# Source tiles of two message-passing layers cut at span bounds instead of group bounds, in a four-layer graph network on Trainium2

## What is computed

```python
# layer 0: per source node, mean of the attributes of its edges, then three dense layers with batch norm
v_e = segment_sum(edge_attr, src) / max(count(src), 1)
# layer 1
agg = segment_sum(x[src], dst) / max(count(dst), 1);  relu((agg + x) @ W.T + b)
# layer 2: messages by edge type
agg = segment_sum(([x[src], x[dst]] @ Wmsg[type] + bmsg[type]), dst) / max(count(dst), 1)
h = [x, agg] @ Wupd + bupd;  x + gelu(norm(h) * gamma + beta)
# layer 3
out = segment_sum((x @ W)[row] * dinv[row] * w * dinv[col], col) + b;  batch_norm(relu(out))
```

## Time and profile before

| | |
|---|---|
| median of 3 runs | 3748.39 us (3743.72 to 3750.21) |
| the profiled execution | 3743.15 us, its span 3741.4 us |
| PE, DVE, ACT, POOL busy | 75%, 67%, 41%, 49% of the span |
| scatter of the edges (POOL, L750) | up to about 1108 us |
| reduce(0) | about 1108 to 1363 us |
| gather(1) with its scatters | about 1468 to 1807 us |
| gather(2), reduce(2) | about 2176 to 2984 us |
| gather(3) with its scatters | about 3078 to 3424 us |

### The profile page before, as it was taken

How to read it: one execution, slowest core, us unless ns; L and a number is a source line. 1 busy time by engine, 2 the same in 40 slices (tenths; PEclk the granted TensorE clock), 3 DMA queues, 4 the chain that set the end, 5 groups by cost and what they waited for, 6 DMA issues and landing times.

```text
span 3741.4 us, 94994 instructions
## 1 busy us (share of the span) xinstructions
PE 2820.6 (75%) x23282; PEld 2453.3 (66%) x23283; DVE 2495.4 (67%) x7099; ACT 1517.8 (41%) x4312; POOL 1847.8 (49%) x2243
## 2 busy tenths in 40 slices
PE   8555544444439986887799689999999958887996
PEld 6232322222229975777799479999899957776995
DVE  7666666666647778555577777777666777554667
ACT  0111100000004445555577543222365348886765
POOL 4777777777763341777433354444521007774000
PEclk9999999999999997999899899999999989998998
DMA  6444444444448943778698035555378807885883
GB/s 216 150 150 141 149 143 146 147 143 149 141 131 285 292 144 104 279 274 280 216 293 274 9 115 175 177 179 183 126 241 248 263 30 273 272 283 194 289 286 123
DMA packets 419041, 721.75 MB, mean 193 GB/s; under 512 B 68624, under 2 KB 198169, under 8 KB 417932
## 3 DMA queue, kind: packets, MB, share of 16 engines
q1 hardware_dynamic: 330492, 494.35, 42.7%
q0 software_dynamic: 88464, 226.43, 16.1%
HBM read 481.26 MB, written 285.09 MB: 205 GB/s over the span
## 4 chain that ended last, share of the span: by engine, by line
PE 42%; POOL 23%; issue 13%; DMA 11%; DVE 5%; ACT 3%; SPq 2%; DVEq 2%; POOLq 1%; ACTq 0%
PE ps L1375 20%; POOL slots L750 19%; PE ps L1408 9%; DMA gbuf<-ring_raw,to_blk 8%; PE ps L1410 5%; POOL gbuf L804 3%; DMA ring_raw<-gbuf 2%; PE ps L1420 2%; PE ps L1250 2%; PE ps L1461 1%; DVEq L501 1%; PE ps L1452 1%; DVE stats L1935 1%; SPq L501 1%; ACT ring_raw L976 1%
## 5 line engine op out<-in xcount | busy, mean ns | idle before, releaser
L804 POOL DMA_INDIRECT gbuf<-ring_raw,to_blk x774 | 754.4, 975 | 727.4 <-DVE ring_raw L1868 257.9
L750 POOL DMA_INDIRECT slots<-ring_raw,idx_edges x782 | 751.4, 961 | 242.2 <-issue 242.2
L1375 PE MATMUL ps<-ring_raw,memory 128*128 128x128 f32 (+2 forms) x6576 | 784.6, 279 | 82.6 <-DVE memory L1836 49.2
L1375 PEld LDWEIGHTS ps<-ring_raw,memory 128*128 128x128 f32 x6576 | 764.5, 193 | 104.9 <-issue 56.3
L1836 DVE TENSOR_TENSOR memory<-dst_lane,lane_ids 128x512 f32<-128x512 f32 x774 | 535.1, 692 | 74.8 <-POOL dst_lane L768 51.7
L1286 PE MATMUL ps<-memory 128*49 128x343 bf16 (+6 forms) x784 | 263.5, 489 | 387.9 <-DVE memory L1732 386.6
L1408 PE MATMUL ps<-memory 128*128 x2752 | 497.8, 273 | 9.9 <-DVE memory L1877 7.5
L1846 DVE TENSOR_TENSOR memory<-memory,ps 128x128 f32 (+2 forms) x1032 | 294.6, 285 | 308.3 <-PE ps L1375 294.8
L935 ACT ACTIVATE memory<-lane_ids,dst_lane 128x128 f32<-128x128 f32 x1032 | 330.3, 392 | 403.2 <-PE ps L1375 246.1
L1410 PE MATMUL ps<-memory 128*128 x2752 | 477.4, 220 | 0.0
L1286 PEld LDWEIGHTS ps<-memory 128*49 128x49 bf16 x784 | 113.9, 159 | 530.4 <-DVE memory L1732 301.6
(11 more groups left out here) (283 smaller groups left out, 4781.6 us busy)
## 6 DMA issues: line engine op xcount, KB each, us to landing
ring_raw<-gbuf SPq DMA_DIRECT2D x669, 268.0 KB, 3.6
ring_raw<-in_edge_attr SPq DMA_DIRECT2D x111, 448.0 KB, 3.8
ring_raw<-slots SPq DMA_DIRECT2D x153, 272.0 KB, 4.1
zr<-lane_rows SPq DMA_DIRECT2D x87, 384.0 KB
zt<-lane_rows SPq DMA_DIRECT2D x87, 384.0 KB
memory<-lane_rows SPq DMA_DIRECT2D x84, 384.0 KB, 4.8
memory<-slots SPq DMA_DIRECT2D x105, 272.0 KB, 4.1
memory<-gbuf SPq DMA_DIRECT2D x105, 268.0 KB, 3.8
```

The source lines that it names most:

```text
L750: pool.indirect_dma_start(edges, bass.IndirectOffsetOnAxis(idx_edges[0:n, u, j:j + 1], 0), edge_rows[0:n, u, j, :], None).then_inc(scatter ...
L804: pool.indirect_dma_start(gbuf, bass.IndirectOffsetOnAxis(to_blk[:, t:t + 1], 0), node_rows[:, r, :], None, bounds_check=NBLK - 1, oob_is_ ...
L1375: ins = pe.matmul(bank(r % 3, width), hots[:, r, j * P:(j + 1) * P], rows[:, j, 0:width], start=j == 0, stop=j == BLK - 1)
```

## The change

In layers 1 and 3 the gather keeps its 258 products of a tile with a group, now called **steps**, but a PSUM bank, an SBUF row and a scatter belong to a **span**: 128 consecutive blocks, whatever groups they are of. There are `SPANS` = 210 of them, in 35 rounds of six. Steps of different groups that meet in one span add up in its bank; the one-hots of blocks of other groups are zero. Because the bank of a step is now data, PE gets for each step a 16-bit word that holds the group's address, the bank, and the number of the next bank, and for each two steps a count of sends to wait for; 27 such values (three rounds) come in one register load. Before the four products of a step, PE does a one-column matmul with `start=True` on the next bank (`new_bank`), so that the products can all be `start=False`. ACT's payload copy in reduce(0) goes to a place by span (its address from a register, twelve loaded for two rounds), and one more copy keeps the target block of each tile; ACT in gather reads the count to wait for from a table, 30 to a load. The payload gets a ninth number, `P_TYPED` (source plus 128 times type less 1), which makes rows of `slots` 137 numbers wide for 136, and POOL keeps both lane tables at once; the four long POOL instructions L792 and L793 after reduce(0) go, three short ones for `to_span` come, and the whole chain waits for the last product of reduce(0). DVE makes the new tables (`span_tables`) behind `at_ready`. Layer 2 keeps its tiles.

```diff
+SPANS = -(-MAXB // P)
+SR = SPANS // RING
+SROUNDS = 3
+SWORDS = RING + RING // 2
+SENDS = 5
...
+STAGED = {1: 0, 2: SPANS, 3: SPANS + TILES}
+
+
 def sends_before(layer):
-    return RR * (layer - 1)
+    return (0, SR, SR + RR, SR + RR + SR)[layer - 1]
...
-PAY = 8
-P_ONE, P_TYPE, P_W, P_DST, P_SRC, P_TO = 0, 1, 4, 5, 6, 7
+PAY = 9
+LIST = PAY - 1
+P_ONE, P_TYPE, P_W, P_DST, P_SRC, P_TYPED, P_TO = 0, 1, 4, 5, 6, 7, 8
...
+            steps.link(pool.tensor_scalar(pay8[:, :, P_TYPED], type_i, float(P), -float(P), ALU.mult, ALU.add))
+            pool.wait_ge(pays_ready, 7)
+            pool.tensor_tensor(pay8[:, :, P_TYPED], pay8[:, :, P_TYPED], pay8[:, :, P_SRC], ALU.add).then_inc(pays_ready, 1)
...
+                        if q == 0:
+                            pool.tensor_tensor(lane_pair[:, :, t * BLK:(t + 1) * BLK],
+                                               rows[:, :, D + P_SRC:D + P_TYPED + 1].rearrange("p k w -> p w k"),
+                                               back[:, q, t:t + 1][:, :, None].broadcast_to([P, 2, BLK]), ALU.add).then_inc(kept, 1)
...
+            pool.wait_ge(products, RING + TILES)
...
-            for t, by in ((0, -P), (2, P)):
-                part = B[:, 0:TILES * BLK].rearrange("p (t k) -> p t k", k=BLK)
-                steps.link(pool.tensor_scalar(part, key_s[:, :, :, P_TYPE + t], float(by), None, ALU.mult))
-                steps.link(pool.tensor_tensor(lane_f, lane_f, part, ALU.add))
...
+            pool.tensor_copy(lanes_t[:, :], edge_w).then_inc(lanes_ready, 1)
+            unused = away[:, 1, 0:SPANS]
+            steps.link(pool.tensor_scalar(unused, key_s[:, :, 0, P_ONE], -NOWHERE, NOWHERE, ALU.mult, ALU.add))
+            steps.link(pool.tensor_tensor(unused, unused, key_s[:, :, 0, P_TO], ALU.add))
+            steps.link(pool.tensor_copy(to_span, unused))
...
+                to = to_blk if layer == 2 else to_span
...
-                for i in range(RR):
+                for i in range(RR if layer == 2 else SR):
...
+            def pay_places(h, n=2 * RING):
+                return nc.values_load_multi_w_load_instructions(
+                    at_pay[:, bass.ds(h * 2 * RING, n)], engines=[ACT_E], min_val=0, max_val=(SPANS - 1) * BLK * PAY,
+                    skip_runtime_bounds_check_because="the tables hold addresses within their tensors")[1]
...
+                    act.copy(to_of[:, bass.ds(i * RING + r, 1)], rows[:, 0, D + P_TO:D + P_TO + 1])
+                    act.wait_ge(pays_kept, i * RING + (RING + r))
+                    act.copy(pays_raw[:, bass.ds(at[r], BLK * PAY)].rearrange("p (k w) -> p k w", k=BLK),
                              rows[:, :, D:ROW_A]).then_inc(pays_kept, 1)
...
+                def counts_of(h):
+                    return nc.values_load_multi_w_load_instructions(
+                        span_steps[layer][:, bass.ds(h * SENDS * RING, SENDS * RING)], engines=[ACT_E], min_val=0,
+                        max_val=RING + GATHERED[3] + TILES,
+                        skip_runtime_bounds_check_because="the tables hold counts of a semaphore")[1]
+
+                def send_round(i, counts):
                     for r in range(RING):
                         at = i * RING + r
-                        act.wait_ge(gathered, i * RING + (RING + base + r + 1))
+                        act.wait_ge(gathered, counts[r])
...
+                counts = counts_of(0)
+                for q in range(SENDS):
+                    send_round(q, counts[q * RING:(q + 1) * RING])
+                with act.Fori(1, SR // SENDS) as h:
+                    counts = counts_of(h)
+                    for q in range(SENDS):
+                        send_round(h * SENDS + q, counts[q * RING:(q + 1) * RING])
...
+                def new_bank(to):
+                    pe.matmul(ps_flat[:, to], ident_h[:, :], none_h, start=True, stop=True, skip_group_check=True)
+
+                def step_words(h, rounds=SROUNDS):
+                    v = nc.values_load_multi_w_load_instructions(
+                        step_lists[layer][:, bass.ds(h * SROUNDS * SWORDS, rounds * SWORDS)], engines=[PE], min_val=0,
+                        max_val=65535, skip_runtime_bounds_check_because="words of 16 bits")[1]
+                    return [v[q * SWORDS:(q + 1) * SWORDS] for q in range(rounds)]
+
+                def in_bounds(v, top):
+                    return nc.s_assert_within(v, 0, top, skip_runtime_bounds_check_because="the words are built so")
+
+                def gather_steps(i, words):
                     for r in range(RING):
+                        at = in_bounds((words[r] & 0x1F8) * 16, (GROUPS - 1) * D)
+                        to = in_bounds(words[r] & 0xE00, (RING - 1) * 512)
+                        upon = in_bounds((words[r] & 7) * 512, (RING - 1) * 512)
+                        if r % 2 == 0:
+                            pe.wait_ge(staged, words[RING + r // 2])
+                        new_bank(bass.ds(upon, 1))
                         pe.wait_ge(src_hots, i * RING + (base + r + 1))
-                        pe.wait_ge(staged, i * RING + (base + r + 1))
                         for j in range(BLK):
-                            ins = pe.matmul(bank(r)[:, j * P:(j + 1) * P], hots[:, r, j * P:(j + 1) * P],
-                                            nodes[:, bass.ds(at[r], D)], start=True, stop=True)
+                            ins = pe.matmul(ps_flat[:, bass.ds(to + j * D, D)], hots[:, r, j * P:(j + 1) * P],
+                                            nodes[:, bass.ds(at, D)], start=False, stop=j == BLK - 1,
+                                            skip_group_check=True)
                         ins.then_inc(gathered, 1)
...
+                    new_bank(slice(0, 1))
+                    with pe.Fori(0, RR // SROUNDS) as h:
+                        for q, words in enumerate(step_words(h)):
+                            gather_steps(h * SROUNDS + q, words)
+                    rest = RR // SROUNDS
+                    for q, words in enumerate(step_words(rest, RR % SROUNDS)):
+                        gather_steps(rest * SROUNDS + q, words)
...
+            groups_on = bank(5, TILES)
+            mark(dve.tensor_scalar(back[:, 0, :], groups_on, -float(P), float(P), ALU.mult, ALU.add))
+            mark(dve.tensor_scalar(at_sum[:, 0, :], groups_on[0:1], float(AW), -float(AW), ALU.mult, ALU.add))
+            mark(dve.tensor_scalar(word_f, groups_on, 8.0, -8.0, ALU.mult, ALU.add))
...
+            def span_tables():
+                link(dve.tensor_scalar(turn_i, span_f, 171.0, None, ALU.mult))
+                link(dve.tensor_scalar(turn_i, turn_i, 10, None, ALU.arith_shift_right))
+                link(dve.tensor_copy(turn_f[:, 1, :], turn_i))
+                link(dve.scalar_tensor_tensor(out=turn_f[:, 0, :], in0=turn_f[:, 1, :], scalar=-float(RING), in1=span_f,
+                                              op0=ALU.mult, op1=ALU.add))
+                link(dve.scalar_tensor_tensor(out=word_f, in0=turn_f[:, 0, :], scalar=512.0, in1=word_f,
+                                              op0=ALU.mult, op1=ALU.add))
+                link(dve.tensor_scalar(turn_f[:, 1, :], turn_f[:, 0, :], RING - 1.5, -float(RING), ALU.is_gt, ALU.mult))
...
+                for layer in (1, 3):
+                    mark(dve.tensor_copy(step_parts[layer][:, :, 0:RING], word_f[32:33].rearrange("p (i r) -> p i r", r=RING)))
+                    mark(dve.tensor_scalar(step_parts[layer][:, :, RING:SWORDS],
+                                           span_f[32:33].rearrange("p (i q two) -> p i q two", q=RING // 2, two=2)[:, :, :, 1],
+                                           float(STAGED[layer] + 2), None, ALU.add))
+                link(dve.tensor_tensor(need_f, tile_ids[:, :], bank(6, TILES), ALU.add))
+                for layer in (1, 3):
+                    mark(dve.tensor_scalar(span_steps[layer], need_f[64:65], float(RING + GATHERED[layer]), None, ALU.add))
+                wait(chain.last())
```

More of the change, by code:

```diff
@@ L58 @@
 HALVES = 2 * RR
+SPANS = -(-MAXB // P)
[3 more added lines that the diff above has]
+SENDS = 5
+assert SR * RING == SPANS and SR % SENDS == 0 and RR % SROUNDS and SPANS + GROUPS - 1 == TILES and SPANS * P <= NBLK
+assert all((t * 171) >> 10 == t // RING for t in range(SPANS))
 SCALAR_HOTS = ((5,), (2, 5), (5,), (2, 5))
@@ L497, in tile_cols @@
         def tile_cols(table, k, i, n=RING, span=RING):
-            return table[0:1, k, bass.ds(i * span, n)] if k is not None else table[0:1, bass.ds(i * span, n)]
+            return table[:, k, bass.ds(i * span, n)] if k is not None else table[:, bass.ds(i * span, n)]
         def loaded(table, k, i, engine, top, span=RING):
@@ L989, in send, with send_typed, send_tiles @@
                     act.wait_ge(lane_rows_out, 32)
[L990 to L995 removed]
+                counts = counts_of(0)
[5 more added lines that the diff above has]
+                        send_round(h * SENDS + q, counts[q * RING:(q + 1) * RING])
+            def send_typed():
```

(14 more changed lines are left out.)

189 lines of the change are left out of this document (102 added, 87 removed).

## The result

The changed kernel takes 4010.26 us (median of 4 runs, 4008.34 to 4013.30) against 3746.32 us before: a ratio of 1.0704, 95% interval 1.0686 to 1.0723. Forecast were 3645 us and a gain. Where the 264 us are is seen in the profiled execution (span 4006.9 us) by stages.

The account below looks back on a forecast made before the run. PE was taken to bound reduce(0), POOL the two gathers at 1.27 us a scatter. Terms -51.5 - 51.5 - 5 + 5 = -103 us took the profiled 3743.15 to 3640, so a median of 3645; range 3605 to 3710.

Parts of the forecast that it names:

- Scatters: Gathers: POOL sends 210 for 258 a layer; as the bound it would need 278 us.
- Rival A: Gathers: new_bank and loads hide better, PE needs 259 us, POOL's 278 decide; median 3619, chance 14%.
- PE's step: Gathers: four products 0.89 us plus new_bank 0.11 make 1.00 us a step, 258 us a layer.
- Register loads: Gathers, PE: 15 loads of 27 values a layer, 1.2 us of pause each, 18 us, bounds 11 and 45.
- seven a layer, each at most 3 us, and the six banks cover that: Gathers: ACT's loads of 30 counts for five rounds would be covered by the six banks.
- PE's registers: Gathers, PE's queue: register work and issue take about 0.85 us a step, hidden behind the step's 1.00.
- the half-way case to rival B: Gathers: PE's queue slightly longer than the products, a step of 1.08 to 1.20 us; median 3670 to 3715, 15%.
- rival B: Gathers: PE's queue becomes the bound, 1.4 us a step, 385 us a layer; median 3833, chance 6%.
- reduce(0), +5: reduce(0): ACT's extra copies and loads +4 us (0 to 25), wider rows of slots +1; together +5.
- Rival C: reduce(0): ACT's register loads hold back SP's refills, 20 to 25 us; 3665 to 3670, chance 8%.
- Edge means, -5: Behind reduce(0): POOL's chain ends earlier, so DVE's groups of seven means are less disturbed, -5 us (0 to -10).
- Tables: Ahead of reduce(0): DVE's rest of 23.9 us covers span_tables, and POOL's scatters aren't delayed; nothing added.

Follow-up runs that it names:

- e12: Kernel before with at_x in steps of eight, so each load begins at a multiple of 16 bytes: 3744.65 us, ratio 0.9997.
- e7: Kernel before with at_x as 16-bit words, one load of 27 (18 used) in three rounds: 3868.54 us, ratio 1.0318.
- e8: Against e5: table of finished 32-bit addresses and a count for two steps, 21 values a round, less PE arithmetic: 3790.2 us, ratio 1.0105.
- e1: Changed kernel with PE's step lists and ACT's counts as 32-bit values, same 27 and 30 to a load: 3951.45 us, ratio 1.054.
- e2: Changed kernel with only PE's step lists 32-bit, ACT's counts still 16-bit: 3988.92 us, one run.
- e5: Changed kernel with 32-bit lists, aligned loads: PE nine values a round at multiples of 48 bytes, ACT 30 at 128: 3834.10 us, ratio 1.0234.
- e6: As e5, but PE loads 27 values once in three rounds, beginning at multiples of 112 bytes: 3822.16 us, ratio 1.0195.
- e9: e5 with two more operations (a mask and an addition) in each PE step: 3893.9 us, ratio 1.0374.

## Why the prediction was wrong

- **What bounds before**: right. e12 and e7 bear it out; POOL is saturated, and of a pause of PE only what the filled banks don't cover counts.
- **Scatters**: 210 sends as said, but POOL's 278 us never decide. Rival A had a chance of 14% and no run near it.
- **PE's step, 0.89 + 0.11 = 1.00 us**: exact, in the changed kernel and in e8.
- **Register loads, "per load 1.2 us of pause ... bounds 0.75 and 3"**: this is the step that failed. The pause is 7.9 us in the mean, the load 8.7 in the median, for 27 values. The row had the price of a value in it, 1.69 us for six, and the prediction treated it as a price of the load; with 0.28 us a value it would have been 7.6 us. Another row spoke against it: `at_msg`, whose 12 values are loaded at once, took 0.89 us. The prediction doesn't ask what makes the two differ (where the address begins; and the new list has narrower values than either). Of its signs, a pause near 1.2 us each three rounds failed at once; the two that it names as deciding, a step of 0.95 to 1.08 us and no uncosted stage moved by over 5 us, both held, and the forecast was wrong all the same. Beside the 15 x 7.9 = 118 us of pauses, for 18 us forecast, stand the 56 us of steps at the lower clock behind them, of which the sum had 2.7 for the first start only.
- **ACT, "seven a layer, each at most 3 us, and the six banks cover that"**: its loads take 7.5 us, and PE waits 1.3 to 4.4 us for ACT six times in gather(1). e1 against e2: 37 us for the 8 of 14 that became short.
- **PE's registers, "about 0.85 us, under the step's 1.00"**: wrong by the price. The 32 ns of the earlier trace rows are the instruction's own time, and the prediction took them for its pace in the queue; there the next one begins 0.09 to 0.15 us later, also where they stand together, and with ten of them the queue needs 1.10 to 1.15 us a step. It is what keeps e5 and e6 at 3834 and 3822: the half-way case to rival B, 3670 to 3715 at 15%, was the nearer one for the arithmetic alone, and by e5 (6 x 1.17 + about 1.7 more at the load for a round, 43 rounds, 375 us) also too low, for the queue is then empty at each load and nothing of it is hidden. The upper end, 3715, doesn't follow from its own terms either: 340 us a layer less 6 of coupling is 46 over the sum, twice, and so 3737.
- **First load of a gather**: not seen apart. In both kernels it begins only when x is ready, so nothing of it is hidden. Before, it took 1.0 us from 1466.6, while DVE wrote its first one-hot, and the products began at 1467.97. Now it takes 6.5 us from 1474.0 and the products begin at 1481.3, 7.6 us behind the `new_bank` that marks x as ready. Its 6.9 us are among the 118:

```profile
1473.72 0.19 PE L1485 MATMUL ps<-none,ident_h 128*128 128x1 bf16 x1 [16.99 <-ACT X L1134]
1480.77 0.18 PE L1485 MATMUL ps<-none,ident_h 128*128 128x1 bf16 x1 [6.86 <-issue]
```

- **reduce(0), +5**: about right. The scatter of the edges ends 3.4 us later, which I had costed at nothing; 3.1 us of it are the 782 scatters themselves (754.5 us busy for 751.4), whose rows are a number wider, and no run tells whether that is the reason. reduce(0) lasts 4.5 us longer (259.6 to 264.1, from POOL's last scatter to PE's last product), with ACT's copies at 0.34 us a tile for 0.13. Rival C didn't happen.
- **Edge means, -5**: nearly nothing came of it. From PE's last product of reduce(0) to ACT's last write of x it is 102.5 us for 103.1, so -0.6. The third group of seven takes 2.04 us for 5.63, but DVE then idles for 1.61 and 1.54 us until ACT's writes: the groups were not alone on the path.
- **Tables**: right. Scatters kept 0.96 and 0.30 us beside `span_tables`, whose work ended 16.5 us before DVE's first one-hot.

Of the 365 us between 3645 and 4010, 175 are in gather(1) (463 us for 288), 184 in gather(3) (478 for 294) and 7 in the other stages. By cause the largest parts are: pauses at loads that are read value by value and the low clock behind them (e6 takes 188 of it away), and the queue's arithmetic with what pauses remain (e6 to the forecast, 177 with those 7). How that second part divides between arithmetic and the reads that remain was not measured apart: e8 takes away 44 of e5's 189, and changes both.

The Trainium skill has a rule that bears on the first part, "Runtime: NRT & Kernel Launch", section "Instruction fetch mechanics": a register load costs about 200 ns for each register, in bulk too. The page tells of registers loaded from HBM; these lists lie in SBUF. As an estimate from that figure, a load of 27 values is 5.4 us and the 387 values of a layer are 77 us, for the 18 of the sum, which would have used up the gain forecast. The trace has 8.7 us, 0.32 us a value, and 0.78 us for 12 values where four cost as one, so by it the figure is too low for the one and too high for the other. The measurement decides.

## What to carry to other kernels

Cost a register load by its values, not as one instruction: here 0.25 to 0.33 us a value, unless they are 32-bit and the load begins at a multiple of 16 bytes, when four come for one. Packing addresses into 16-bit words to save loads makes both sides dearer: the load is not shorter, and the unpacking is queue time, which counts once a step's register instructions, at about 0.1 us each, take longer than its products. And when a change lifts the bound of a stage, everything that was hidden under it (loads, restarts at the lower clock) is to be counted anew at its full price.

## What the runs showed of the hardware

- A load of n values from SBUF to registers: 27 of 16 bits 8.7 us (PE) and 30 of them 7.5 (ACT); 9 of 16 bits 2.98; 27 of 32 bits 7.7 to 9.1 in e1 where the load doesn't begin at a multiple of 16 bytes, 2.3 to 4.5 in e1 and e6 where it does; 12 of 32 bits at multiples of 48 bytes 0.78 (ACT) and 0.89 (PE); 8 of 32 bits 0.71. The same load varies: the first of a gather takes 6.5 us where later ones take 8.1 to 10.0.
- A register instruction that isn't fused with its neighbour costs PE's queue about 0.1 us (e9's one more: 1.22 and 1.33 us a step for 1.13 and 1.21), though its own row says 32 ns.
- In the changed kernel PE's products ran at the lower clock (2.07 us for 1.14) for two to four steps behind each of the 34 pauses of over 4 us. Of the pauses of 0.5 to 2.2 us, 12 of 77 had such steps behind them in e5, 18 of 78 in e8 and 28 of 79 in e9.
